# Third attention stage of an eight-stage transformer kernel: the causal mask as two constant rows in the stacked operands and four 64x64 triangle products, in place of one 128-row mask product

## The chip, the cores and the metric

One core of one Trainium2 chip runs the whole program. The metric is the device time of one execution in microseconds (us). Engines are named as the profile names them: PE is the matrix engine (TensorE), PEld its weight loads, DVE the vector engine, ACT the scalar engine, POOL GpSimd, SP the engine that issues the DMAs.

## The reference, cut to what matters

The reference is four layers, each an attention and a feed-forward part with modulated layer norms, over 16 batches of 256 tokens with 256 features. The change touches the attention of the second layer (`L1_attn`, the third of eight stages), a differential attention with 32 score heads of 8 features:

```python
q = (x @ Wq).reshape(b, t, 2 * H, HD).transpose(0, 2, 1, 3) * scaling
k = (x @ Wk).reshape(b, t, 2 * H, HD).transpose(0, 2, 1, 3)
scores = jnp.einsum('bhqd,bhkd->bhqk', q, k)
causal = jnp.triu(jnp.full((t, t), -jnp.inf, dtype=jnp.float32), 1)
aw = jax.nn.softmax((scores + causal).astype(jnp.float32), axis=-1)
lam = jnp.exp(jnp.sum(lq1 * lk1)) - jnp.exp(jnp.sum(lq2 * lk2)) + LAMBDA_INIT
aw = aw.reshape(b, H, 2, t, t)
aw = aw[:, :, 0] - lam * aw[:, :, 1]
attn = jnp.einsum('bhqk,bhkd->bhqd', aw, v)
```

## The kernel before, in words

The eight stages run one after another, each over the 16 batches, in software-pipelined slots (`slots`). Each engine has its own program, and semaphores order them. A slot i of this stage holds on PE the maxima of batch i, most of the exponentials' scores of batch i - 1, and projections, transposes and the output product of neighbouring batches.

**Stacks.** q and k are split into three bf16 parts. `l1a_sync` writes the parts to DRAM, `l1a_stack_sync` reads them back into `QS` and `KS` (per parity of the batch) as 48 rows for one half of the heads, on partitions 0 to 47, and 48 for the other half, on partitions 64 to 111. One bf16 product over 48 rows gives an f32-like score. Three more rows of `QS` take the row maxima (negated, in three bf16 parts), against ones in `KS`; `l1a_max_sync` sends them there from `maxT`, in two halves of a batch. The other rows are zero in `QS`.

**Pairs.** Scores are worked on in pairs of PSUM banks of 512 columns: bank `pr` = 0 takes its operands from partitions 0 to 63, bank 1 from 64 to 127. Each batch has 12 maxima pairs (`max_pair(b, o, n)`, o = 0 to 3, n = 0 to 2, written Mon here, as M00 or M32) and 12 exponential pairs (`exp_pair`, Eon). A pair is either four blocks of 128 columns a bank (M with n = 0, E with n = 2: "wide mask", since a mask of 512 columns goes over the bank) or two blocks of 256 columns a bank (all the others: "narrow mask", 256 columns). The mask is a product of the identity (`ident_b`, 128x128) with `later4` or `earlier4` (a 128x128 triangle of -1e30, repeated), added to the bank in PSUM. In a wide pair it comes ahead of the scores, in a narrow one behind them. So a narrow pair has on PE 4 score matmuls and 2 mask matmuls, a wide pair 2 mask matmuls and 8 score matmuls.

**Who frees whom.** The three banks 1 to 3 serve M pairs, 4 to 6 E pairs. DVE reduces each M bank to maxima (`maxima`, L2185); ACT takes the exponential of each E bank (`exps`, L2104). An M pair waits on PE until DVE has done the first bank of the M pair before it; an E pair waits until ACT has done the first bank of the E pair before it. E00 and E20 wait for the maxima's rows (`max_ready`), M00 for the stacks (`stack_ready`).

**PE's order in a slot** is written by hand in `slot` of `l1a_tensor`. V is `values` (products on column strips of 32), P a projection, bt a transpose by token, nT and MT other transposes:

M00, E12, P(k), E20, M01, V1, E21, M02, E22, P(q), E30, M10, V2, E31, M11, E32, M12, nT, M20, V3, MT first, M21, M22, P(v), bt 0 to 2, M30, bt 3, out, E00, M31, E01, M32, E02, next tokens' transposes, E10, V0, MT second, E11, and the next slot.

**Other orders.** ACT: between E12 and E20 it evicts k (L2118, L2119), between E20 and E21 it copies V1's result (`l_oT`, L2110), and so on; between E02 and E10 it writes the next `hT` (L517); ahead of E11 it copies V0's result and `maxT` (L2093). DVE: behind M22 comes `by_token` (L2193, L2195) and `subtract`, then M30, the gated output (L533), M31, M32. POOL makes the parts of q, k and of the maxima. SP's slot order is `l1a_sync(i + 1)`, maxima's first half of i, stacks of i + 1, maxima's second half of i. `l1a_pads`, which POOL runs in the second stage's first four slots, sets the constant rows by memset and counts `a_zero` to 4.

Of the kernel before, what the change touches and what calls it, by code (L numbers as in the profile page):

```python
# [16 lines left out]
P = 128  # L17
B = 16
T = 256
# [119 lines left out]
def layout(**inputs):  # L139

    a = {k: np.asarray(v) for k, v in inputs.items()}
    f = np.float32
    k = np.arange(P)
    two = lambda w: np.ascontiguousarray(w.reshape(KH, P, -1).transpose(1, 0, 2))
    out = {"x": a["L0_attn_x"].reshape(B, TT, P, D)}
    out["c"] = np.ascontiguousarray(np.stack([two(a[f"L{i}_c"].T) for i in range(LAYERS)], 1))
    out["wmod"] = np.stack([a[f"L{i}_wmod"] for i in range(LAYERS)])
    ident = np.eye(P, dtype=f)
    out["ident"] = ident

    for n in "qkvo":
        out[f"l0_w{n}"] = two(a[f"L0_attn_W{n}"])
    out["l0_wg1"], out["l0_wg2"] = two(a["L0_attn_Wg1"]), a["L0_attn_Wg2"]
    ld = a["L0_attn_log_decay"]
    out["l0_ld"] = ld
    out["l0_nw"] = np.ascontiguousarray(a["L0_attn_norm_w"].reshape(KH, P).T)
    age = np.arange(T)[None, :] - k[:, None]
    out["l0_age"] = np.maximum(age, 0).astype(f)
    out["causal"] = (age >= 0).astype(f)
    out["l0_side"] = (k[:, None] // HD % 2 == np.arange(2)[None, :]).astype(f)  # L160
    age = age[:, 0:P]

    pad = np.zeros((FT * P - INTER, D), np.int32)
    down = np.concatenate([a["L0_ffn_down_idx"].T, pad]).reshape(FT, P, D).transpose(1, 0, 2)
    out["l0_idx"] = np.concatenate([two(a["L0_ffn_gate_idx"].T).reshape(P, -1), two(a["L0_ffn_up_idx"].T).reshape(P, -1),
                                    down.reshape(P, -1)], 1)
    out["l0_lut"] = a["L0_ffn_lut"]

    out["l2_b"] = two(a["L2_attn_B"].T)
    out["l2_c"] = np.ascontiguousarray(a["L2_attn_C"].T)  # L170
    out["l2_d"] = np.ascontiguousarray(a["L2_attn_D"].reshape(KH, P).T)

    out["l3_wqkv"], out["l3_wo"] = two(a["L3_attn_w_qkv"]), two(a["L3_attn_w_out"])
    out["l3_dec"] = np.ascontiguousarray(np.repeat(a["L3_attn_decay_param"], HD).reshape(KH, P).T)
    out["l3_head"] = (k[:, None] // HD == np.arange(P // HD)[None, :]).astype(f)

    for n in "qkvo":
        w = a[f"L1_attn_W{n}"]
        if n in "qk":
            w = w.reshape(D, 8, KH, 2, 8).transpose(0, 2, 3, 4, 1).reshape(D, D)  # L180
        out[f"l1_w{n}"] = two(w)
    out["lam_v"] = np.stack([np.stack([a[f"L1_attn_lq{i}"], a[f"L1_attn_lk{i}"]]) for i in (1, 2)])
    bf = mybir.dt.np(BF16)
    low = np.where(age < 0, np.float32(LOW), np.float32(0))
    out["ident_b"] = ident.astype(bf)
    out["later4"] = np.ascontiguousarray(np.broadcast_to(low.T[:, None], (P, 4, P))).astype(bf)
    out["earlier4"] = np.ascontiguousarray(np.broadcast_to(low[:, None], (P, 4, P))).astype(bf)

    out["l1_we"] = np.ascontiguousarray(a["L1_ffn_expert_w"].reshape(E, KH, P, D).transpose(2, 1, 0, 3))
    out["l1_gw"], out["l1_eb"] = two(a["L1_ffn_gate_w"].T), a["L1_ffn_expert_b"]  # L190

    out["l2_la"], out["l2_w"] = two(a["L2_ffn_lora_A"].reshape(P, D).T), two(a["L2_ffn_weight"].T)
    out["l2_rw"] = two(a["L2_ffn_router_w"].T)
    out["l2_lb"] = np.ascontiguousarray(a["L2_ffn_lora_B"].transpose(0, 2, 1)).reshape(P, D)
    out["l2_sel"] = (np.arange(E)[:, None] == k[None, :] // (P // E)).astype(f)

    rows = lambda w: w.transpose(1, 0, 2).reshape(D, NS)
    out["l3_sw"] = two(rows(a["L3_ffn_select_weight"]))
    out["l3_up"] = two(np.concatenate([rows(a["L3_ffn_lora_update"]), np.zeros((D, E), f)], 1))
    out["l3_md"], out["l3_db"], out["l3_mdr"] = two(a["L3_ffn_select_mean_diff"].T), two(a["L3_ffn_debias_w"].T), a["L3_ffn_select_mean_diff"]  # L200
    out["l3_cs"] = np.stack([a["L3_ffn_imp_center"], a["L3_ffn_imp_slope"]], 1)
    out["l3_dg"] = np.concatenate([a["L3_ffn_lora_degen"].transpose(0, 2, 1).reshape(NS, D), a["L3_ffn_bias_w"]])
    blk = (np.arange(NS)[:, None] // (NS // E) == np.arange(E)[None, :]).astype(f)
    out["l3_blk"] = np.concatenate([blk, np.zeros((P - NS, E), f)])
    out["l3_own"] = np.concatenate([blk, np.zeros((E, E), f)])
    out["l3_e72"] = np.ascontiguousarray(np.concatenate([blk, np.eye(E, dtype=f)]).T)
    out["l3_tail"] = (np.arange(NS + E) >= NS).astype(f)[:, None]
    out["l3_one"] = np.ones((P, E), f)
    out["rank"] = np.broadcast_to(np.arange(E, 0, -1).astype(f), (P, TT, E)).copy()
    return {"in_" + k: v for k, v in out.items()}  # L210


def build(nc, ins, y_out, first=0, last=8):
    ctx = ExitStack()
    with ctx:
# [1614 lines left out]
        def l1a_tensor(pe, pl, s):  # L1830
            psum_free(pe, pl)
            pe.wait_ge(w_in[2], 16 * len(weights[2]))
            pe.wait_ge(setup["a_wo"], 1)
            pe.wait_ge(setup["a_zero"], 4)

# [29 lines left out]
            def half_rows(x, pr, g, a, b_, rows):  # L1867
                return x[64 * pr:64 * pr + rows, g, a:b_]

            def max_pair(b, o, n):  # L1870
                u = 6 * o + 2 * n
                q, k = QS[b.par], KS[b.par]
# [5 lines left out]
                    pe.wait_ge(*s.max(b - 1, 23))  # L1878
                banks = [bank(1 + (u + pr) % 3) for pr in range(2)]
                if n == 0:  # L1880
                    for pr in range(2):
                        pe.matmul(banks[pr], ident_b[:, :], later4[:, :, :], start=True, stop=False)
                    for j in range(4):
                        for pr in range(2):
                            last_ = pe.matmul(banks[pr][:, j * P:(j + 1) * P], half_rows(q, pr, 4 * o + j, 0, P, M_ROW),  # L1885
                                              half_rows(k, pr, 4 * o + j, 0, P, M_ROW), start=False, stop=j == 3)
                            if j == 3:
                                last_.then_inc(s.max_ps.sem, 1)
                else:
                    for j in range(2):  # L1890
                        for pr in range(2):
                            g = 4 * o + 2 * (n - 1) + j
                            pe.matmul(banks[pr][:, j * T:(j + 1) * T], half_rows(q, pr, g, P, T, M_ROW),  # L1893
                                      half_rows(k, pr, g, 0, T, M_ROW), start=j == 0, stop=False)
                    for pr in range(2):
                        pe.matmul(banks[pr].rearrange("p (j k) -> p j k", j=2)[:, :, P:T], ident_b[:, :], later4[:, 0:2, :],  # L1896
                                  start=False, stop=True).then_inc(s.max_ps.sem, 1)

            def max_T(b, half_):
                pe.wait_ge(*s.mparts(b, half_ + 1))  # L1900
# [21 lines left out]
            def exp_pair(b, o, n):  # L1922
# [11 lines left out]
                if n < 2:  # L1934
                    for j in range(2):
                        for pr in range(2):
                            g = 4 * o + 2 * n + j
                            pe.matmul(banks[pr][:, j * T:(j + 1) * T], half_rows(k, pr, g, 0, P, 64),  # L1938
                                      half_rows(q, pr, g, 0, T, 64), start=j == 0, stop=False)
                    for pr in range(2):  # L1940
                        pe.matmul(banks[pr].rearrange("p (j q) -> p j q", j=2)[:, :, 0:P], ident_b[:, :], earlier4[:, 0:2, :],  # L1941
                                  start=False, stop=True).then_inc(s.score.sem, 1)
                else:
                    for pr in range(2):
                        pe.matmul(banks[pr], ident_b[:, :], earlier4[:, :, :], start=True, stop=False)  # L1945
                    for j in range(4):
                        for pr in range(2):
                            last_ = pe.matmul(banks[pr][:, j * P:(j + 1) * P], half_rows(k, pr, 4 * o + j, P, T, 64),
                                              half_rows(q, pr, 4 * o + j, P, T, 64), start=False, stop=j == 3)
                            if j == 3:  # L1950
                                last_.then_inc(s.score.sem, 1)

            def values(b, o):
                pe.wait_ge(*s.prob(b, 6 * o + 6))
# [371 lines left out]
            slots(pool, slot, -3, LOOP2, B + 1)  # L2326

        N_STACK = 4
        M_ROW = 8 * N_TERMS

        def l1a_sync(sp, pl, s, b):

# [9 lines left out]
        def l1a_stack_sync(sp, pl, s, i):  # L2342
# [5 lines left out]
            for c in (1, 0):  # L2348
                if not c or not (i - 1).ok:
                    sp.wait_ge(*scratch_ready(i, c))  # L2350
                for r in range(2):
                    to = (QS, KS)[c][i.par][64 * r:64 * r + M_ROW, :, :].rearrange("p g t -> p (g t)")
                    sp.dma_start(to, qk_dram[i.par, c, r].rearrange("n (d g) x -> (n d) (g x)", d=8)).then_inc(stack_in[i.par], 16)

        def l1a_max_sync(sp, pl, s, b, half_):
# [109 lines left out]
        def _(sp):  # L2465
# [20 lines left out]
            for p in range(first, last):  # L2486
                pl = p - first
                def slot(i):
                    if i.ok and p != 2:
                        gate_load(sp, pl, sigs[pl], i)  # L2490
                    if i.reg is None and i.off == 1 and pl + 1 < len(sigs):
                        if pl:
                            sp.wait_ge(*sigs[pl - 1].x(Idx(None, B - 1)))
# [70 lines left out]
```

## Time and profile before

| | |
|---|---|
| median of 3 runs | 2099.39 us (2097.16 to 2099.85) |
| profiled execution | 2101.8 us, its span in the trace 2100.0 us |
| mean granted PE clock | 0.936 of full speed |
| busy: PE, DVE, ACT, POOL | 1850.9, 1373.0, 741.1, 895.8 us |
| the third stage | score products from 670 to 1235 us of the span |

The profile is one execution. A busy time is a sum over the span; PE's is modelled, since matmuls are pipelined and a single one takes longer than its share of a stream, so what a group of matmuls costs is read from the start of one group to the start of the next. The timeline merges neighbouring instructions of one kind on one row, with their count.

### The profile page before, as it was taken

What the parts mean: (1) busy time and instruction counts of PE and PEld (TensorE: products, weight loads), DVE (VectorE), ACT (ScalarE), POOL (GpSimd) and SP (SyncE); (2) the same over time, 40 slices, a digit from 0 to 9 for tenths busy, and PEclk for the clock granted to TensorE, in tenths of its full rate; (3) what the DMA queues carried; (4) which work ended last, traced back from release to release, by engine and by line L of the source; (5) the groups of instructions that cost most, each with busy time, mean ns of one, the idle gap of its engine ahead of it and who ended that gap; (6) DMA issues with size and microseconds to landing.
All of it is one profiled execution on the core that took longest, in us unless ns stands there. A gap on an engine that the chain in (4) does not pass through costs nothing.

```text
span 2100.0 us, 40010 instructions
## 1 busy us (share of the span) xinstructions
PE 1850.9 (88%) x13400; PEld 1270.9 (61%) x13400; DVE 1373.0 (65%) x3587; ACT 741.1 (35%) x1511; POOL 895.8 (43%) x965
## 2 busy tenths in 40 slices
PE   8999999689995999999999968998967888998887
PEld 5555555489993455555555436676756666885443
DVE  4767677465552556565656537888845776886775
ACT  2544444112221465555555531111122223443332
POOL 0345454565653254545454332233333223663233
PEclk7999999799998999999999988999999888999887
DMA  6100000100003745454545300000011000000111
GB/s 230 52 9 5 7 5 9 31 9 8 10 10 68 158 87 106 89 103 90 100 89 103 68 11 9 9 7 7 10 33 43 15 13 17 14 16 13 35 37 40
DMA packets 68177, 93.34 MB, mean 44 GB/s; under 512 B 9852, under 2 KB 62316, under 8 KB 64748
## 3 DMA queue, kind: packets, MB, share of 16 engines
q1 hardware_dynamic: 68076, 92.01, 19.3%
q8 instruction: 61, 1.00, 0.2%
q14 instruction: 40, 0.33, 0.1%
HBM read 61.70 MB, written 29.49 MB: 43 GB/s over the span
## 4 chain that ended last, share of the span: by engine, by line
PE 68%; DVE 19%; issue 6%; POOL 2%; ACT 2%; DMA 2%; SPq 1%; DVEq 1%; POOLq 0%; ACTq 0%
PE PS L1020 16%; PE PS L1965 3%; PE PS L668 3%; PE PS L1841 3%; PE PS L725 3%; PE PS L1175 3%; DVE negmax L2185 2%; PE PS L741 2%; PE PS L507 2%; DVE xn L497 2%; PE PS L722 2%; PE PS L1893 2%; PE PS L1896 2%; PE PS L1945 1%; PE PS L1938 1%
## 5 line engine op out<-in xcount | busy, mean ns | idle before, releaser
L2185 DVE TENSOR_REDUCE negmax<-PS 128x2 f32<-128x512 f32 (+1 forms) x384 | 246.9, 684 | 211.2 <-PE PS L1885 106.0
L538 POOL TENSOR_TENSOR X<-X,y_sb 128x512 f32 (+1 forms) x128 | 165.2, 1291 | 150.1 <-DVE y_sb L533 145.1
L533 DVE TENSOR_TENSOR y_sb<-PS,ga_sb 128x512 f32<-128x512 f32 x96 | 66.2, 690 | 179.0 <-PE PS L769 50.1
L1020 PE MATMUL PS<-we_hi,h_parts 128*128 128x512 f32 x512 | 179.7, 412 | 0.0
L497 DVE TENSOR_SCALAR xn<-X,mv,rs 128x256 f32 (+1 forms) x256 | 155.3, 648 | 22.4 <-POOL rs L490 21.2
L517 ACT ACTIVATE hT<-PS,modT 128x256 f32<-128x256 f32 x256 | 130.0, 559 | 105.6 <-PE PS L507 104.6
L2104 ACT ACTIVATE pw<-PS 128x512 f32<-128x512 f32 x256 | 139.0, 600 | 75.2 <-PE PS L1941 75.2
L488 POOL TENSOR_TENSOR rs<-mv,eps 128x2 f32<-128x2 f32 x128 | 26.6, 208 | 296.3 <-DVE mv L481 296.1
L1020 PE MATMUL PS<-l_h_parts,lut_hi 128*128 128x256 f32 (+1 forms) x768 | 145.5, 291 | 6.7 <-POOL l_h_parts L1143 6.7
L1509 DVE SCALAR_TENSOR_TENSOR l_acc<-PS,rt_g,l_acc 128x256 f32<-128x256 f32 x256 | 106.1, 475 | 30.6 <-PE PS L1020 25.5
L1020 PEld LDWEIGHTS PS<-l_h_parts,lut_hi 128*128 128x128 f32 (+1 forms) x768 | 117.8, 184 | 9.6 <-issue 5.4
L1020 PEld LDWEIGHTS PS<-we_hi,h_parts 128*128 128x128 f32 x512 | 99.1, 194 | 26.5 <-issue 5.9
L1020 PE MATMUL PS<-l_h_parts,lut_lo 128*128 128x256 f32 (+1 forms) x384 | 110.3, 287 | 0.0
L507 PE MATMUL PS<-ident,xn 128*128 128x128 f32 x512 | 82.1, 284 | 31.6 <-DVE xn L497 30.8
L1020 PE MATMUL PS<-we_lo,h_parts 128*128 128x512 f32 x256 | 102.9, 402 | 0.0
L1175 PE MATMUL PS<-hT,l_wqkv 128*128 128x256 f32 x384 | 94.3, 397 | 4.9 <-ACT hT L517 4.0
L1089 ACT ACTIVATE l0f_act<-PS 128x256 f32<-128x256 f32 x96 | 36.8, 383 | 175.1 <-PE PS L1020 175.1
L490 POOL TENSOR_TENSOR rs<-rs,half 128x2 f32<-128x2 f32 x128 | 94.0, 734 | 10.0
L476 DVE BATCH_NORM_STATS2 st<-X 128x6 f32 (+1 forms) x256 | 95.1, 413 | 1.1 <-DMA X<-in_x 0.9
L1152 POOL TENSOR_TENSOR l0f_hid_parts<-l0f_hid,l0f_hid_parts 128x256 fp32r<-128x256 f32 x96 | 72.2, 753 | 50.5 <-DVE l0f_hid_parts L1014 50.0
L507 PEld LDWEIGHTS PS<-ident,xn 128*128 128x128 f32 x512 | 58.4, 143 | 57.0 <-DVE xn L497 38.5
L988 POOL TENSOR_TENSOR l_ms<-l_ms,half 128x32 f32<-128x32 f32 x16 | 87.1, 5442 | 1.3
(270 smaller groups left out, 4383.2 us busy)
## 6 DMA issues: line engine op xcount, KB each, us to landing
ga_sb<-ga_dram SPq DMA_DIRECT2D x128, 128.0 KB, 2.9
qk_dram<-qk_parts SPq DMA_DIRECT2D x64, 192.0 KB, 2.8
KS<-qk_dram SPq DMA_DIRECT2D x32, 384.0 KB, 5.7
QS<-qk_dram SPq DMA_DIRECT2D x32, 384.0 KB, 9.5
qk_dram<-qk_parts SPq DMA_DIRECT2D x64, 128.0 KB, 2.8
wmod<-in_wmod SPq DMA_DIRECT2D x4, 1536.0 KB, 14.0
qk_dram<-qk_parts SPq DMA_DIRECT2D x64, 64.0 KB, 2.5
y_out<-X SPq DMA_DIRECT2D x16, 256.0 KB, 2.2
```

Of the source, the lines that this page charges most:

```text
L476: last_ = dve.bn_stats(st6[b.par][:, t, :], xb(b)[:, t, :])
L490: pool.tensor_tensor(rs[b.par][:, :], rs[b.par][:, :], half[:, 0:TT], ALU.pow).then_inc(s.rstd.sem, 1)
L497: last_ = dve.tensor_scalar(xn[b.par][:, t, :], xb(b)[:, t, :], mv[b.par][:, t, 0:1], rs[b.par][:, t:t + 1], ALU.subtract, ALU.mult)
L507: last_ = pe.transpose(PS[:, 0, kh * T + t * P:kh * T + (t + 1) * P], xn[b.par][:, t, kh * P:(kh + 1) * P], ident[:, :])
L517: last_ = act.activation(hT[b.par][:, kh, :], PS[:, 0, kh * T:(kh + 1) * T], ACT.Identity, bias=modT[:, sub, 0, kh, bass.ds(b.n, 1)], scal ...
L538: pool.tensor_tensor(xb(b), xb(b), y_sb[b.par][:, :, :], ALU.add).then_inc(s.x.sem, 1)
L988: pool.tensor_tensor(ms_sb[:, :], ms_sb[:, :], half[:, 0:TT * HEADS], ALU.pow).then_inc(s.rn.sem, 1)
L1020: last_ = pe.matmul(out, x.bitcast(F32R), y.bitcast(F32R), start=start and n == 0, stop=stop and n == 2)
L1175: last_ = pe.matmul(bank(1 + n)[:, m * T:(m + 1) * T], l3_wqkv[:, kh, n * D + m * P:n * D + (m + 1) * P], hT[b.par][:, kh, :], start=kh == ...
L1509: dve.scalar_tensor_tensor(l1_acc[b.par][:, t, :], bank(1 + (2 * q + t) % 4)[:, e * D:(e + 1) * D], rt_g[b.par][:, t, x_:x_ + 1], l1_acc[b ...
L2104: act.activation(to.rearrange("p a n -> p (a n)"), bank(4 + (2 * n + pr) % 3), ACT.Exp).then_inc(s.prob.sem, 1)
L2185: dve.tensor_reduce(to, src, AX.X, ALU.max, negate=True).then_inc(s.max.sem, 1)
```

## The change

The stacks get two constant rows below the 48 (rows 48 and 49 of each half). Row t of `QS` is 1 in the first 64 tokens of token tile t, row t of `KS` is -1e30 in the last 64 tokens of it. So the score product itself masks the upper right 64x64 block of each 128x128 diagonal block. `M_ROW` grows from 48 to 50, and the maxima's three rows move down by two. What is left to mask are the two 64x64 triangles on the diagonal. `triangles` adds them with four matmuls a pair, each of 64 rows by 64 columns of the array, with the identity's diagonal quarter as weights: quarter 0 for bank 0 and quarter 1 for bank 1, then quarter 1 for bank 0 and quarter 0 for bank 1. They come behind the scores in every pair. The rows are sent by eight DMAs (`l1a_cut_sync`) from SP's queue in the second stage, at the slot of batch 14, into both parities; PE waits for them (`a_pad`) at the head of the third stage.

```diff
+    cut_q, cut_k = np.zeros((2, HEADS, T), f), np.zeros((2, HEADS, T), f)
+    for t in range(TT):
+        cut_q[t, :, t * P:t * P + P // 2] = 1
+        cut_k[t, :, t * P + P // 2:(t + 1) * P] = LOW
+    out["cut"] = np.stack([cut_q, cut_k]).astype(bf)
...
             pe.wait_ge(setup["a_zero"], 4)
+            pe.wait_ge(setup["a_pad"], 16 * 8)
...
+            def triangles(banks, tri, n, done):
+                for half_ in range(2):
+                    for pr in range(2):
+                        h = pr ^ half_
+                        r0, r1 = 64 * h, 64 * h + 64
+                        last_ = pe.matmul(banks[pr][r0:r1, :, r0:r1], ident_b[r0:r1, r0:r1], tri[r0:r1, 0:n, r0:r1],
+                                          start=False, stop=True)
+                        if half_ == 1:
+                            last_.then_inc(done.sem, 1)
...
                 if n == 0:
-                    for pr in range(2):
-                        pe.matmul(banks[pr], ident_b[:, :], later4[:, :, :], start=True, stop=False)
                     for j in range(4):
                         for pr in range(2):
-                            last_ = pe.matmul(banks[pr][:, j * P:(j + 1) * P], half_rows(q, pr, 4 * o + j, 0, P, M_ROW),
-                                              half_rows(k, pr, 4 * o + j, 0, P, M_ROW), start=False, stop=j == 3)
-                            if j == 3:
-                                last_.then_inc(s.max_ps.sem, 1)
+                            pe.matmul(banks[pr][:, j * P:(j + 1) * P], half_rows(q, pr, 4 * o + j, 0, P, M_ROW),
+                                      half_rows(k, pr, 4 * o + j, 0, P, M_ROW), start=j == 0, stop=False)
+                    triangles([x.rearrange("p (j k) -> p j k", j=4) for x in banks], later4, 4, s.max_ps)
...
-                    for pr in range(2):
-                        pe.matmul(banks[pr].rearrange("p (j k) -> p j k", j=2)[:, :, P:T], ident_b[:, :], later4[:, 0:2, :],
-                                  start=False, stop=True).then_inc(s.max_ps.sem, 1)
+                    triangles([x.rearrange("p (j k) -> p j k", j=2)[:, :, P:T] for x in banks], later4, 2, s.max_ps)
...
-        M_ROW = 8 * N_TERMS
+        S_ROW = 8 * N_TERMS
+        M_ROW = S_ROW + TT
+        def l1a_cut_sync(sp):
+            sp.wait_ge(setup["a_zero"], 4)
+            for i in range(2):
+                for c, to in enumerate((QS, KS)):
+                    for r in range(2):
+                        sp.dma_start(to[i][64 * r + S_ROW:64 * r + M_ROW, :, :], ins["cut"][c]).then_inc(setup["a_pad"], 16)
...
+                    if i.reg is None and i.off == B - 2 and p == 1:
+                        l1a_cut_sync(sp)
```

`exp_pair` is changed in the same way, with `earlier4` and the first 128 of each 256 columns.

## Rows read from the trace of the kernel before

**Rows 1.** Busy time in a stretch of 40 us: start:end, length, each engine's, clock, DMA

```profile
1000.00:1040.00 40.00, 38.67 (x403) 23.18 (x402) 25.61 (x54) 20.06 (x39) 17.49 (x20) 1.00 0.54 103
```

**Rows 2.** Waits of PE, 700 to 1200 us: total us, times, longest

```profile
PE PS L1893 <- DVE negmax L2185: 14.2, 28, 0.7
PE PS L1882 <- DVE negmax L2185: 3.8, 14, 0.7
```

**Rows 3.** Timeline of the eviction of q and k, two slots apart

```profile
843.22 0.60 ACT L2118 ACTIVATE qk<-PS 128x512 f32<-128x512 f32 x1 [0.99 <-PE PS L1841]
...
912.84 0.60 ACT L2118 ACTIVATE qk<-PS 128x512 f32<-128x512 f32 x1 [0.99 <-PE PS L1841]
```

**Rows 4.** PE's groups by shape, whole span: count, busy us, mean ns, idle before

```profile
L1896 PE MATMUL PS<-later,ident_b 128*128 128x256 bf16 x256 | 51.0, 282 | 0.0
...
L1882 PE MATMUL PS<-later,ident_b 128*128 128x512 bf16 x128 | 39.6, 392 | 22.0 <-DMA QS<-qk_dram 17.3 <-DVE negmax L2185 4.7
```

**Rows 5.** Timeline of PE, one slot: start us, length us, instructions

```profile
1008.87 0.59 PE L1945 MATMUL PS<-earlier,ident_b 128*128 128x512 bf16 x2
...
1013.11 0.39 PE L1941 MATMUL PS<-earlier,ident_b 128*128 128x256 bf16 x2
1013.34 0.59 PE L1882 MATMUL PS<-later,ident_b 128*128 128x512 bf16 x2
1013.87 0.40 PE L1885 MATMUL PS<-KS,QS 48*128 48x128 bf16 x8
1014.20 0.61 PE L1945 MATMUL PS<-earlier,ident_b 128*128 128x512 bf16 x2
...
1018.96 0.61 PE L1965 MATMUL PS<-pw,l_vpad 128*32 128x256 f32 x8
1019.39 0.40 PE L1967 MATMUL PS<-pz,l_vpad 128*32 128x128 f32 x8
1019.73 0.39 PE L1938 MATMUL PS<-QS,KS 64*128 64x256 bf16 x4
1020.05 0.39 PE L1941 MATMUL PS<-earlier,ident_b 128*128 128x256 bf16 x2
...
1021.02 0.61 PE L1945 MATMUL PS<-earlier,ident_b 128*128 128x512 bf16 x2
...
1032.63 0.39 PE L1893 MATMUL PS<-KS,QS 48*128 48x256 bf16 x4
...
1034.03 0.39 PE L1893 MATMUL PS<-KS,QS 48*128 48x256 bf16 x4 [0.68 <-DVE negmax L2185]
```

**Rows 6.** Weight loads by shape, whole span, columns as before

```profile
L1643 PEld LDWEIGHTS PS<-hT,l_sw 128*64 128x64 f32 x64 | 7.9, 144 | 12.9 <-issue 8.1 <-DVE l_c L1739 2.0 <-ACT hT L517 0.4
...
L1896 PEld LDWEIGHTS PS<-later,ident_b 128*128 128x128 bf16 x256 | 14.6, 97 | 27.8 <-issue 27.8
...
L1685 PEld LDWEIGHTS PS<-l_sq,l_blk 128*8 128x8 f32 x32 | 1.6, 90 | 7.5 <-issue 7.4
```

**Rows 7.** Timeline, the first weight loads of V1

```profile
1018.28 0.16 PEld L1965 LDWEIGHTS PS<-pw,l_vpad 128*32 128x32 f32 x8 [0.21 <-issue]
```

**Rows 8.** The chain that ended last, in order of time: start us, us

```profile
1004.37 0.27 DVE l_rl L2193
...
1007.58 0.69 DVE negmax L2185
1008.32 0.39 PE PS L1893 x4
...
1009.84 0.59 ACT pz L2104
1010.48 0.39 PE PS L1938 x4
```

**Rows 9.** Timeline of ACT in the same slot

```profile
1020.37 1.08 ACT L2104 ACTIVATE pw<-PS 128x512 f32<-128x512 f32 x2
```

**Rows 10.** Timeline of PE where the stage runs out

```profile
1224.20 0.39 PE L1938 MATMUL PS<-QS,KS 64*128 64x256 bf16 x4 [1.66 <-DMA QS<-maxT]
```

More of the change, by code:

```diff
@@ L1939, in exp_pair @@
                                       half_rows(q, pr, g, 0, T, 64), start=j == 0, stop=False)
-                    for pr in range(2):
-                        pe.matmul(banks[pr].rearrange("p (j q) -> p j q", j=2)[:, :, 0:P], ident_b[:, :], earlier4[:, 0:2, :],
-                                  start=False, stop=True).then_inc(s.score.sem, 1)
-                else:
-                    for pr in range(2):
-                        pe.matmul(banks[pr], ident_b[:, :], earlier4[:, :, :], start=True, stop=False)
+                    triangles([x.rearrange("p (j q) -> p j q", j=2)[:, :, 0:P] for x in banks], earlier4, 2, s.score)
+                else:
                     for j in range(4):
                         for pr in range(2):
[L1948 to L1951, printed above, removed]
+                            pe.matmul(banks[pr][:, j * P:(j + 1) * P], half_rows(k, pr, 4 * o + j, P, T, 64),
+                                      half_rows(q, pr, 4 * o + j, P, T, 64), start=j == 0, stop=False)
+                    triangles([x.rearrange("p (j q) -> p j q", j=4) for x in banks], earlier4, 4, s.score)
             def values(b, o):
@@ L2351, in l1a_stack_sync @@
                 for r in range(2):
-                    to = (QS, KS)[c][i.par][64 * r:64 * r + M_ROW, :, :].rearrange("p g t -> p (g t)")
+                    to = (QS, KS)[c][i.par][64 * r:64 * r + S_ROW, :, :].rearrange("p g t -> p (g t)")
                     sp.dma_start(to, qk_dram[i.par, c, r].rearrange("n (d g) x -> (n d) (g x)", d=8)).then_inc(stack_in[i.par], 16)
```

## The prediction

> **What bounds the kernel now.** I read first the table of stages over time. In a stretch of the third stage PE is busy 38.67 of 40 us, at full granted clock, DVE 25.6, ACT 20.1, POOL 17.5 [rows 1]. So this stage runs at PE's pace, unlike what an average over eight stages would tell, and work taken off PE can be worth time. Next the list of waits: between 700 and 1200 us the maxima's pairs wait for DVE 14.2 + 3.8 = 18.0 us in 42 places [rows 2], 1.3 us for each of some 14 batches. These waits are where a faster PE will lose part of its gain. Then the distance of one instruction over two slots: 912.84 - 843.22 = 69.62, so a batch takes 34.81 us [rows 3]. There are 16 batches, and 15 slots (1 to 15) hold both a full set of M pairs and a full set of E pairs.
>
> **What one pair costs on PE.** The mean of a mask product (282 and 392 ns, [rows 4]; as many again stand for `earlier4`) holds the array's latency. What it costs in a stream is the distance of starts [rows 5]. Narrow mask, then wide mask, both on the full array: 13.34 - 13.11 = 0.23 us, which I take as 0.22. Wide mask, then scores: 13.87 - 13.34 = 0.53. Eight 128-column scores, then a mask: 14.20 - 13.87 = 0.33. Four 256-column scores, then a mask: 20.05 - 19.73 = 0.32. Now 0.22 us for 2 x 256 columns is 2.4 GHz, so 2 x 512 columns are 0.43 and the 0.53 holds 0.10 to 0.11 more; the scores' 0.33 is 0.22 (half their columns, since the two 64-row halves run at once) and again 0.11. In the values' products, which use four strips of 32 columns, a second group starts after 0.43 (19.39 - 18.96, same shape), and scores behind them after 0.34, 0.12 more than their own 0.22. So each change of the array's split costs 0.11 us, and staying in one costs nothing. This is the term that speaks against the change.
>
> Before: a narrow pair is 0.22 + 0.11 + 0.22 = 0.55, and 0.11 more if the next group does not use the full array. A wide pair is 0.43 + 0.11 + 0.22 = 0.76, and 0.11 more if the next is not a score group.
>
> After: the scores are unchanged (50 rows of weights instead of 48 change no column). The triangles are four matmuls of 128 (narrow) or 256 columns (wide). If the two on different quarters run at once, each pair takes two steps: 0.11 or 0.22 us. No row shows a split in both directions; rows show it by rows (scores) and by columns (values: four strips, [rows 5]), so I take it. Their weights have 64 columns in bf16, for which there is no row either. Bounds: a bf16 load of 128 columns has 97 ns, an f32 load of 64 columns 144 [rows 6]. So the first, which nothing hides, costs 0 to 0.05 more; later ones run beside matmuls. I take 0.02, nearer the bf16 row. A narrow pair then is 0.22 + 0.11 + 0.11 + 0.02 + 0.11 = 0.57, say 0.56, a wide one 0.67, always with the change at its end, because triangles are followed by something else everywhere.
>
> So on PE a narrow pair gains 0.09, but loses 0.01 where the mask ran on into a full-array group (E11, M02, E30, M11, M12, M22, M32: seven of sixteen). A wide one gains 0.19 (eight a batch; E32, ahead of M12, 0.08). M20 and M30 also get 0.11 of a new change in front, behind nT and bt. PE's work falls by 9 x 0.09 - 7 x 0.01 + 7 x 0.19 + 0.08 - 0.22 = 1.93 us a batch. By plain columns it would have been 16 x 0.11 + 8 x 0.21 = 3.4.
>
> **What of it reaches the end.** I go through PE's order and ask at each pair which wait ends last.
> - bt 3 to M32: a chain on DVE. The last token transposes are read at 1004.37; by_token, subtract, two M30 maxima, the gated output and the first of M31 follow back to back, until 1007.58 + 0.69, and M32 starts at 1008.32 [rows 8]. PE only has out and three pairs in these 3.95 us. E00, M31, E01: nothing gained.
> - M32: -0.01. E02 to E10: bank 0's exponential starts 0.97 behind E02 (1009.84 - 1008.87, [rows 8, 5]) and E10 0.64 later. With triangles bank 0 is ready after 0.22 + 0.11 + 0.02 + 0.11 (its second triangle's start) + 0.33 for latency and hand-over (before, its last score started at 0.43 + 0.11 + 0.16 = 0.70 and 0.27 followed; a product twice as long adds 0.05), 0.79. Gain 0.18.
> - E10, E11, M00: from E02's exponentials ACT runs without a gap (two of E02, `hT`, two of E10, V0's copy, `maxT`) up to E11's, and E12 waits for the first of these. Nothing.
> - E12: 0.19. E20 and M01: 0.09 each.
> - E21, M02: V1's copy holds up E21's exponential till 1020.37, 0.64 behind E21 [rows 9, 5]; 0.60 later the wide E22 may start, and did, at 1021.02. Nothing.
> - E22: 0.19. E30: -0.01. M10: 0.19.
> - E31, M11, E32: the same copy, nothing; then E32's 0.08 to 0.11, I take 0.11 with M11's earlier start for M12.
> - M12, nT to M20: M20 waits for M12's first reduction as M22 does for M21's below; nothing. M20: 0.19.
> - M21 to M22: 34.03 - 32.63 = 1.40 [rows 5]: bank 0 ready (0.65), one reduction (0.69), hand-over. Bank 0 is as late as before, since its second triangle is third in order (0.22 + 0.11 + 0.02 + 0.05 and latency, before 0.22 + 0.11 + 0.11). Nothing.
> - M22: -0.01. M30: 0.19 - 0.11 = 0.08.
>
> Sum: -0.01 + 0.18 + 0.19 + 0.18 + 0.19 - 0.01 + 0.19 + 0.11 + 0.19 - 0.01 + 0.08 = 1.28 us a batch, two thirds of PE's 1.93. Times 15 slots: 19.2. Slots 0 and 16 hold only M or only E pairs and wait for DVE and ACT; a few wide pairs there lead such a chain, 0.2 each and 0.4 where the clock is half: 1.3 us. Together 20.5 us.
>
> **What is added elsewhere.** Eight DMA issues of 16 KB on SP at the second stage's batch 14. Even at 1 us each they hold SP for 8 us; behind them stands only the gate load of batch 15, which has to wait for DVE's output of an earlier batch anyway, and then SP has nothing to issue until the first q and k parts. `a_zero` was counted up in slots 0 to 3 of that stage. Lower bound 0, upper bound 1 us if batch 15's gate came late; I take 0. PE's wait on `a_pad` is met tens of us before. 48 more matmuls and 48 more loads a batch: eight loads and eight matmuls already pass in 0.22 us [rows 5], so issue does not bind. E20 waits for `maxT`'s rows by DMA: where the stage runs out it stood 1.66 us for them [rows 10], in steady slots not. E12's gain brings E20 nearer to them; if it is lost there, 0.19 x 15 = 3 us. The bound for the forecast's range.
>
> Against the profiled execution: 2101.8 - 20.5 = 2081.3. Its time is 2.4 above the median of the runs, so the forecast is 2099.4 - 20.5 = 2079. Own range: no cost of the first load gives 0.02 x 17 places more, -26, 2074; its upper bound takes 0.03 x 17 = 0.5 a batch away, -12, and E20's 3 us more, 2090.
>
> **The rivals.**
> (a) Loads set the pace of a quarter. A 64-column f32 load takes 144 - 90 = 54 ns longer than one of 8 columns [rows 6]. If bf16 loads on quarters cost as much and run one behind another, each group of triangles takes 4 x 0.054 = 0.22 us or more: narrow pairs lose 0.02 (or 0.12), wide ones gain 0.15, and bank 0 is ready 0.1 us later in the six chains that wait for it. Summed over the same places this is -0.07 us a batch: 2100, no change. For it: nothing shows a bf16 load on part of the columns. Against it: V1's first eight loads, on four strips, span 0.16 us together [rows 7] where one alone takes 90 ns or more [rows 6], so the other seven start within 0.07 us and loads on different strips overlap. The Trainium skill, page TensorEngine Tiling (Array Packing), section Restrictions, says that column tiling turns off fast weight load, and its page TensorE: Matmul & The Clock Gate, section LDWEIGHTS, gives a load as columns / 1.2 GHz, by which four loads in a row are an estimated 213 ns. By that rule without overlap the sum would be that of this rival; if the loads overlap, that of the forecast. No row here shows bf16 loads of this shape.
> (b) Slower: the four triangles don't run at once. Then they take 0.22 and 0.43 us, what the full masks took, and nothing pays for the ten more changes of split a batch (60 for 50). A narrow pair is 0.66, a wide one 0.87 to 0.89. Gains turn to losses of 0.02 to 0.14 at the places above (0.11 where the mask ran on, and 0.11 each in front of M20 and M30 where these don't wait), and bank 0 is ready 0.07 later: 1.1 us a batch, 16 us, 2116. It decides for slower as soon as the second and third triangle's overlap is less than about half of the columns. For it: quarter 1 is used twice in a row, quarter 0 only at the ends, and bank 0 gets its second triangle while its first may still be draining. The Trainium skill, the same tiling page, section Restrictions and Gotchas, says that different row tiles must not use one PSUM bank at a time; the order here is meant for that, and no row shows the case.
> (c) The change from scores to triangles is free, as both keep 64-row halves. Then each pair drops another 0.11, and 0.11 at each of 14 places where scores follow triangles. On the path: 1.9 us a batch more, 3.1 in all, 2051. For it only that no row shows such a change; all that rows show cost 0.11.
>
> **Chances.** Forecast 0.70 (with E20's DMA and dearer first loads in it), (a) 0.10, (b) 0.12, (c) 0.08. The range leaves out (b) and (c), 0.20, and takes in (a): 2062 to 2101. The lower end lies below the forecast's own 2074, for a case between it and (c). A measurement of this kernel tells about 0.2%, 4 us, from no change. Faster: 0.70 + 0.08 = 0.78; the same 0.10; slower 0.12.
>
> **What would show it.** Triangles in the timeline: x4 with the next group 0.22 to 0.25 us (narrow) or 0.33 to 0.36 (wide) behind them is the forecast; 0.33 and 0.53 is (b); 0.33 to 0.37 for both is (a); scores to triangles in 0.22 is (c). The eviction of q and k repeats after 67.1 us for two slots instead of 69.6. PE's waits for DVE between 700 and 1200 us grow from 18 to some 23, and waits for ACT ahead of E12, E22 and E32 appear. PE's busy share falls. M21 to M22 stays 1.40, bt 3 to M32 3.95. The forecast goes wrong if triangles are serial, if waits for DMA at E20 or M00 grow past 1 us, or if the thinner work lets the granted clock fall below 1.00 between 720 and 1200 us.

## The result, and the profile after

The changed kernel takes 2105.99 us (median of 12 runs, 2101.78 to 2112.04) against 2098.07 us for the kernel before in the same session (12 runs). The ratio is 1.0041, 95% interval 1.0028 to 1.0054: slower by 0.4%, where 1.0% faster was forecast. The profiled execution has a span of 2110.1 us.

PE's timeline of a slot of the changed kernel comes first (start, length, instructions); it answers to [rows 5].

```profile
1000.64 0.41 PE L1883 MATMUL PS<-later,ident_b 64*64 64x256 bf16 x4
1000.98 0.64 PE L1973 MATMUL PS<-pw,l_vpad 128*32 128x256 f32 x8
...
1002.42 0.39 PE L1951 MATMUL PS<-QS,KS 64*128 64x256 bf16 x4
1002.74 0.30 PE L1883 MATMUL PS<-earlier,ident_b 64*64 64x128 bf16 x4
1002.97 0.39 PE L1908 MATMUL PS<-KS,QS 50*128 50x256 bf16 x4
1003.29 0.30 PE L1883 MATMUL PS<-later,ident_b 64*64 64x128 bf16 x4
1003.73 0.40 PE L1957 MATMUL PS<-QS,KS 64*128 64x128 bf16 x8
...
1008.12 0.39 PE L1908 MATMUL PS<-KS,QS 50*128 50x256 bf16 x4
...
1009.53 0.39 PE L1908 MATMUL PS<-KS,QS 50*128 50x256 bf16 x4 [0.79 <-DVE negmax L2193]
...
1013.98 0.66 PE L1986 MATMUL PS<-ident,l_oT 128*128 128x128 f32 x4
...
1018.63 0.39 PE L1908 MATMUL PS<-KS,QS 50*128 50x256 bf16 x4 [0.40 <-DVE negmax L2193]
...
1019.19 0.40 PE L1957 MATMUL PS<-QS,KS 64*128 64x128 bf16 x8
...
1020.61 0.39 PE L1951 MATMUL PS<-QS,KS 64*128 64x256 bf16 x4
```

Four wide triangles with the change of split behind them take 0.34 us (1000.98 - 1000.64), four narrow ones 0.23 (1002.97 - 1002.74), scores before triangles 0.32 (1002.74 - 1002.42). So the quarters do run at once, as the forecast had it. E21 to E22 is 1.31 (1003.73 - 1002.42), M21 to M22 1.41 (1009.53 - 1008.12), E02 to E10 1.42 (1020.61 - 1019.19): also as forecast. From bt 3 to M32 PE takes 4.65 us (1018.63 - 1013.98). The kernel before has these two rows, which give 4.64:

```profile
1003.68 0.65 PE L1978 MATMUL PS<-ident,l_oT 128*128 128x128 f32 x4
...
1008.32 0.39 PE L1893 MATMUL PS<-KS,QS 48*128 48x256 bf16 x4 [0.31 <-DVE negmax L2185]
```

The loads of the triangles, from the table of groups by shape, answer to [rows 6]; the second row shows the four loads of one group in the timeline:

```profile
L1883 PEld LDWEIGHTS PS<-later,ident_b 64*64 64x64 bf16 x768 | 26.9, 106 | 35.6 <-issue 29.2
...
1002.74 0.14 PEld L1883 LDWEIGHTS PS<-earlier,ident_b 64*64 64x64 bf16 x4 [0.21 <-issue]
```

A 64-column bf16 load has 106 ns, 9 more than a full one (in a stretch at full clock, 780 to 870 us, 104 against 97). Now the same timeline 20 us further on, at the jump from the second slot of PE's loop back to the first (M00 is the first pair of the loop body), and the table of stretches for the slots before and across such a jump, whose last columns are clock, DMA share and GB/s:

```profile
1023.14 0.30 PE L1883 MATMUL PS<-earlier,ident_b 64*64 64x128 bf16 x4
1026.24 0.40 PE L1901 MATMUL PS<-KS,QS 50*128 50x128 bf16 x8 [2.80 <-issue]
1026.57 0.41 PE L1883 MATMUL PS<-later,ident_b 64*64 64x256 bf16 x3
1030.31 0.37 PE L1883 MATMUL PS<-later,ident_b 64*64 64x256 bf16 x1 [3.33 <-issue]
1030.61 0.61 PE L1957 MATMUL PS<-QS,KS 64*128 64x128 bf16 x8
1031.14 0.64 PE L1883 MATMUL PS<-earlier,ident_b 64*64 64x256 bf16 x4
1031.71 3.29 PE L1847 MATMUL PS<-hT,l_wk 128*128 128x256 f32 x8
```

```profile
809.65:843.11 33.46, 31.46 (x416) 19.09 (x412) 21.97 (x43) 19.50 (x38) 17.47 (x21) 1.00 0.52 101
843.11:884.91 41.80, 33.71 (x416) 20.27 (x412) 22.04 (x43) 19.51 (x39) 18.86 (x23) 0.92 0.43 84
```

Both stretches run from one eviction of k to the next. A slot without a jump takes 33.46 us, against 34.81 before [rows 3] and 33.53 forecast. A slot behind a jump takes 41.80, 8.34 more. Of this, 2.80 + 3.33 = 6.13 us are two pauses of PE which wait for nothing that the profile shows ("issue"): one at the jump's target, the other in the middle of a group of four triangles, ahead of its last one. Of the other 2.2 us, 1.3 are seen in the projection of k, which takes 3.29 us where without a jump it takes 1.99: the granted clock behind the pauses is lower (0.92 over the slot). The list of PE's waits, 700 to 1200 us, answers to [rows 2]:

```profile
PE PS L1908 <- DVE negmax L2193: 16.9, 28, 0.8
PE PS L1883 <- issue: 9.7, 3, 3.3
PE PS L1901 <- issue: 8.8, 3, 3.2
PE PS L1901 <- DVE negmax L2193: 3.4, 14, 0.8
PE PS L1901 <- DMA QS<-qk_dram: 1.4, 1, 1.4
```

Three times two pauses, and PE's loop over slots 4 to 11 in two-slot bodies jumps back three times. Three jumps cost about 3 x 8.34 = 25 us (the three slots take 41.80, 41.74 and 41.62). None of the waits of the kernel before was of this kind and length. What PE waits for is seen in the table of DMA queues. From 885 to 1095 us it has this row for the kernel before:

```profile
q8 instruction: 1, 0.02, 0.0%
```

and this one for the changed kernel:

```profile
q8 instruction: 24, 0.39, 0.8%
```

The queue that brings instructions (packets, MB, share) moved one packet of 16 KB in this stretch for the kernel before, and even that one starts at 1087.5 us, behind the loop's last pass, which ends at 1082.9. In the changed kernel it moved 24, nine of them in the round from 947 to 1023 us. In 14 us around the pauses above, 1020 to 1034 us, it is three:

```profile
q8 instruction: 3, 0.05, 1.6%
```

Two of the three lie in the pauses. They start at 1023.6 and 1028.0 us and take 1.0 us each, and PE goes on 1.7 and 1.3 us behind their ends, at 1026.24 and 1030.31.

So in the kernel before PE held its loop body of two slots and did not fetch it again. The change adds 2 matmuls and 2 loads to each of the 24 pairs of a slot, 192 instructions to the body of two slots. From then on PE fetches its body in every round, and stands still at the jump until the first pieces are there. The Trainium skill, page Runtime: NRT & Kernel Launch, section Instruction fetch mechanics, says that PE's instruction memory holds 2048 instructions, is refilled in blocks of 16 KiB or 256 instructions, and that a taken branch to a target outside the current window of two such pages forces a fetch before execution can go on. The packets of 16 KB and the pauses at the jump agree with it. The two pages do not: the kernel before jumps back over some 1560 instructions, and no packet moves. Nor is a body of 1757 held, although it is shorter than 2048; the experiments below narrow the limit down.

### The profile page after: what moved, and what is told of

It is laid out like the page before. It is cut to its first block, busy times and chain, and to the rows that moved or that the text cites. A ratio compares the mean times of both kernels' runs of the same rounds, so it can differ in the third digit from the quotient of the medians.

```text
span 2110.1 us, 41555 instructions
## 1 busy us (share of the span) xinstructions
PE 1829.3 (87%) x14168; PEld 1278.6 (61%) x14168; DVE 1375.5 (65%) x3587; ACT 741.9 (35%) x1511; POOL 895.3 (42%) x965
## 4 chain that ended last, share of the span: by engine, by line
PE 64%; DVE 19%; issue 7%; ACT 4%; POOL 2%; DMA 2%; SPq 1%; DVEq 1%; ACTq 0%; POOLq 0%
PE PS L1025 16%; PE PS L1883 4%; PE PS L1847 3%; PE PS L673 3%; PE PS L1973 3%; PE PS L1180 3%; PE PS L730 3%; DVE negmax L2193 2%; PE PS L746 2%; PE PS L512 2%; PE PS L727 2%; DVE xn L502 2%; PE PS L697 1%; ACT pw L2112 1%; PE PS L774 1%
```

## The experiments

Throughout, "body" is PE's loop body of two slots. By the built program it has 1565 PE instructions before and 1757 after the change, if a bf16 product or a transpose counts as a load and a matmul, any other f32 product as two of each, and every register or semaphore instruction as one. Three fused register instructions are counted together with their 8 parts; counted once each, they make it 1557 and 1749. This count serves for differences; it need not be what the memory holds to the instruction.

**PE's loop written out (u_after, u_before).** The same edit on the changed kernel and on the kernel before:

```diff
-            slots(pe, slot, -2, LOOP2, B + 1)
+            for i in range(-2, B + 2):
+                slot(Idx(None, i))
```

> The changed kernel, with PE's loop over the slots 4 to 11 of the third stage written out (20 slots in a row, no jump; the other engines keep their loops). Theory (code): PE's loop body of two slots has grown by 192 instructions, is no longer held, and is fetched again at each of three jumps back, about 8.3 us each (41.8 against 33.5 us from one eviction of k to the next). Then the pauses of 2.8 and 3.3 us go away everywhere, no slot takes longer than 33.6 us, and the time falls by some 25 us against the changed kernel: 2080 us, 0.991 of the kernel before. Rival (split): the pauses come from the 64x64 split or the order of the triangles; they stay wherever they were, since the instructions and their order are the same: 2106. Rival (clock): the clock falls by itself now and then under thinner work: time stays above 2095.

> The kernel before, with PE's loop of the third stage written out in the same way. Theory (code): its body was held and the jump back showed no pause, so nothing is gained: 2098 us, within 0.2% of the kernel before; 34.8 us a slot. Rival: the loop itself (register arithmetic for the waits, the jump) already cost something, then this is faster by what it cost, and the part of it in the other run's gain is not the larger body's.

Measured: the changed kernel without PE's loop 2084.68 us, ratio to the kernel before 0.9927 (0.9900 to 0.9954), 21 us below the changed kernel (24.4 between the stages of the two profiles, where 25 were expected). The kernel before without PE's loop 2097.70 us, ratio 0.9997 (0.9983 to 1.0011). In u_after's waits between 640 and 1260 us the long pauses are gone; the one "issue" entry that is left stood in the kernel before too:

```profile
PE PS L1908 <- DVE negmax L2194: 22.5, 38, 0.8
PE PS L1901 <- DMA QS<-qk_dram: 18.6, 3, 16.7
...
PE PS L1951 <- issue: 0.9, 1, 0.9
```

The same triangles in the same order make no pause when there is no jump, so neither the split nor the clock by itself is the cause. In the kernel before, the loop as such cost nothing that can be measured.

**The instructions without the triangles (cut_before).** The kernel before, each mask product in two halves, in both kinds of pair and for maxima and exponentials; here for the wide maxima pairs:

```diff
-                    for pr in range(2):
-                        pe.matmul(banks[pr], ident_b[:, :], later4[:, :, :], start=True, stop=False)
+                    for h in range(2):
+                        for pr in range(2):
+                            pe.matmul(banks[pr][:, h * T:(h + 1) * T], ident_b[:, :], later4[:, 2 * h:2 * h + 2, :],
+                                      start=h == 0, stop=False)
```

> The kernel before, with each mask product cut in two of half the columns: the same columns on the full array, no triangles, no constant rows, but four mask products a pair and so the same number of PE instructions in the loop body as in the changed kernel. Theory (code): three jumps back with two pauses of about 3 us each and some half clock behind them, 20 to 25 us slower than the kernel before: 2118 to 2123 us. Rival (split): without a 64x64 split there is no pause and the time stays at 2098 to 2100.

Measured: 2123.24 us, ratio 1.0113 (1.0088 to 1.0137), 25 us slower than before. PE's timeline at one of its jumps:

```profile
955.03 0.40 PE L1946 MATMUL PS<-earlier,ident_b 128*128 128x128 bf16 x4
958.16 1.03 PE L1883 MATMUL PS<-later,ident_b 128*128 128x256 bf16 x4 [2.74 <-issue]
959.13 0.61 PE L1887 MATMUL PS<-KS,QS 48*128 48x128 bf16 x8
962.29 1.03 PE L1952 MATMUL PS<-earlier,ident_b 128*128 128x256 bf16 x4 [2.55 <-issue]
```

Full-array products, no constant rows, no new DMA: the same two pauses, at the jump's target and twelve products behind it (eleven in the changed kernel), in a body that is as long. This run decides for the code.

**How long the body may be (wide_only, cut_few).** In wide_only, the changed kernel's narrow pairs get the full mask back (cut to `max_pair`; the same in `exp_pair`):

```diff
-                    triangles([x.rearrange("p (j k) -> p j k", j=2)[:, :, P:T] for x in banks], later4, 2, s.max_ps)
+                    for pr in range(2):
+                        pe.matmul(banks[pr].rearrange("p (j k) -> p j k", j=2)[:, :, P:T], ident_b[:, :], later4[:, 0:2, :],
+                                  start=False, stop=True).then_inc(s.max_ps.sem, 1)
```

> The changed kernel with triangles in the wide pairs only (8 a batch); the narrow pairs add the full 256-column mask product as before (the constant rows mask their block a second time). The loop body has 64 instructions more than before instead of 192. Theory (code): if the limit lies above that, there is no pause, and the wide pairs bring their 1.0 us a batch, 15 us in all: 2083 us. If the limit lies below, the same three pauses: 2108. Rival (split): pauses appear with the wide triangles too (in the changed kernel the second pause stood ahead of the last triangle of a wide pair): 2108.

cut_few is cut_before with the cut in the wide maxima pairs alone (the diff above and nothing else).

> The kernel before, with only the masks of the four wide maxima pairs a batch cut in two: 32 instructions more in the loop body than before, where 64 more (wide triangles only) gave the full pauses. Theory (code) with a limit at the body's size: either no pause, 2098 us, and the limit lies between 32 and 64 more, or the full three, 2122, and it lies within 32 of the kernel before. A gradual price would show as something between, 2102 to 2108.

Measured: wide_only 2109.75 us, ratio 1.0052 (1.0035 to 1.0069), with six pauses:

```profile
PE PS L1901 <- issue: 18.3, 6, 3.5
```

cut_few 2099.88 us, ratio 1.0002 (0.9986 to 1.0019), with one instruction packet between 885 and 1095 us. So 32 instructions more are free and 64 more cost all three jumps: it is a step, between 1597 and 1629 in the count above, and no gradual price. The kernel before lay 2 to 4% below it. In wide_only a slot without a jump takes 33.86 us: the wide triangles bring 0.95 us a batch, the narrow ones 0.40.

Length is not all in which these bodies differ, and the second pause shows it. In the changed kernel it stands behind the eleventh product of M00, in wide_only behind the third:

```profile
949.44 0.28 PE L1901 MATMUL PS<-KS,QS 50*128 50x128 bf16 x3 [2.87 <-issue]
953.23 0.48 PE L1901 MATMUL PS<-KS,QS 50*128 50x128 bf16 x5 [3.51 <-issue]
```

That is 8 products or 16 instructions earlier. By the built programs wide_only's body begins 240 instructions earlier too, because the slots ahead of the loop carry the same edit. 240 + 16 = 256, so the second pause fits a border between pieces of 256 instructions, one packet each. From this border each body's place can be worked out (an estimate; with the fused instructions counted once). The bodies of before, cut_few and cut_outside (below) touch seven pieces, the latter two with room for 9 and 5 instructions more; those of wide_only, cut_before and the changed kernel touch eight. So the limit may be one of length, or one of seven pieces, in which the place where the body begins counts as well. No run separates the two.

**Where the body lies (cut_outside).** As cut_before, but the masks are cut only in the slots that are written out (one line of the edit; it sets in how many parts a mask is added):

```diff
+        CUT = CUT_E = lambda b: 2 if b.reg is None else 1
```

> The kernel before, with all masks cut in two as in the run that had the pauses, but only in the slots outside the loop; the loop body is as long as before and lies elsewhere in the program. Theory (the size of the body decides): no pause at the jumps, 2098 to 2100 us. Rival (where the body lies, or the length of the whole program): pauses at the jumps, above 2110 us.

Measured: 2099.88 us, ratio 1.0008 (0.9989 to 1.0026), 2 instruction packets in the stretch where cut_before has 24. So the program's length does not decide, nor does this shift of the body's place, by some 100 instructions within its pieces. It still leaves the body in seven of them.

**One jump (one_jump).** The changed kernel with

```diff
-            slots(pe, slot, -2, LOOP2, B + 1)
+            slots(pe, slot, -2, (4, 8), B + 1)
```

> The changed kernel with PE's loop over the slots 4 to 7 only and the other slots written out: the same large body, one jump back instead of three. Theory (code): each jump back costs 8.3 us, so this stands one jump above the kernel without a loop (2084.7) and two below the changed kernel (2106): 2089 to 2093 us, pauses at one place only, at about 870 us of the span. Rival (something else that the long loop brings, such as DMA traffic over the stage): not in steps of one jump; several pauses or none.

Measured: 2090.80 us, ratio 0.9959 (0.9941 to 0.9976), and one set of pauses in PE's timeline:

```profile
874.58 0.40 PE L1901 MATMUL PS<-KS,QS 50*128 50x128 bf16 x8 [3.23 <-issue]
...
878.10 0.37 PE L1883 MATMUL PS<-later,ident_b 64*64 64x256 bf16 x1 [2.79 <-issue]
```

Without a jump 2084.7, with one 2090.8, with three 2106.0: 6 to 8 us each. The slot with the jump takes 42.02 us, 8.6 more than the one before it.

**Which triangles are worth it (u_wide, u_mix).** u_after gained 14 to 15 us where 20.5 were forecast. From the first eviction of k to that of batch 3 it takes 96.92 us, the kernel before 94.27. wide_only took only 92.29. So two more kernels, both with PE's loop written out: u_wide has wide triangles only, u_mix narrow ones too, but not in the first three batches (cut to `max_pair`; the same in `exp_pair`):

```diff
+                    if b.off < 3:
+                        for pr in range(2):
+                            pe.matmul(banks[pr].rearrange("p (j k) -> p j k", j=2)[:, :, P:T], ident_b[:, :], later4[:, 0:2, :],
+                                      start=False, stop=True).then_inc(s.max_ps.sem, 1)
+                        return
```

> The changed kernel with triangles in the wide pairs only and PE's loop written out. With the loop this kernel showed 33.86 us a slot (all triangles: 33.46), and reached batch 3 some 4.6 us earlier than the kernels with all triangles did, where the first slots ran partly at half clock. If both stay: no pauses, 0.40 x 12 slots dearer and 4.6 cheaper than all triangles without a loop, so about the same, 2084 us. If the narrow triangles are worth what PE saved on them by columns alone, it stands 10 us or more above, 2095.

> As the run before, but with narrow triangles too from batch 3 on; batches 0 to 2 have the full narrow masks. Theory (the first slots' loss comes from the narrow triangles there: PE catches up with the DMA of the stacks and with DVE, waits, and its clock falls): it keeps the 4.6 us at the start and the 33.46 us a slot: about 2080 us, 4 us below all triangles without a loop. Rival (the loss at the start is chance of the clock): the same as all triangles, 2084.

Measured: u_wide 2079.74 us, ratio 0.9911 (0.9893 to 0.9929); u_mix 2082.38 us, ratio 0.9913 (0.9891 to 0.9936). Both beat the kernel before by 0.9% and the changed kernel by more; between them and u_after the intervals don't decide. From the first eviction of k to the last transposes by token the profiles take 593.8 us before, 603.6 in the changed kernel, 579.2 in u_after, 577.8 in u_wide, 576.1 in u_mix. Each is one execution, so the order of the last three is not shown. Up to batch 3 u_mix needs 92.6 us, as forecast, and its slots take 33.45. Over all profiles this start takes 96.9 to 97.3 us in the three kernels with narrow triangles in it (the changed kernel, one_jump, u_after), 92.3 to 93.1 in the three with wide ones alone there, and 93.6 to 95.4 in the five without triangles. The 4 us are thus the narrow triangles of the first batches. The rows bear on how they come about, but do not settle it: in the first slots PE waits for the stacks' DMA and for DVE anyway, and the granted clock falls to 0.68 of full speed in u_after and one_jump (the level of 1.2 GHz for part of the stretch), and to 0.73 in the changed kernel, where u_mix and u_wide stay at 1.00. It was 1.00 in the kernel before, but 0.83 in u_before and cut_few, which have no triangles either. The table of stretches, for u_after:

```profile
726.00:736.00 10.00, 8.19 (x89) 4.04 (x88) 6.71 (x15) 5.21 (x10) 4.74 (x7) 0.68 0.55 95
```

and for the kernel before:

```profile
726.00:736.00 10.00, 8.39 (x99) 3.74 (x97) 6.90 (x17) 6.78 (x14) 4.84 (x7) 1.00 0.64 103
```

and for u_mix:

```profile
726.00:736.00 10.00, 9.01 (x113) 4.53 (x114) 7.39 (x16) 7.43 (x16) 5.75 (x7) 1.00 0.52 86
```

## Why the prediction was wrong

- **The step that failed** is "48 more matmuls and 48 more loads a batch: eight loads and eight matmuls already pass in 0.22 us [rows 5], so issue does not bind." The rate was right: no group of triangles is held up within a slot. But the instructions were costed only by their rate, at nothing, and they also have a length. The loop body grew past what PE holds, and three jumps cost 25 us (41.80 - 33.46 each). With this term the forecast of -20.5 us becomes +4.5; measured are +8 by the medians and +9.8 between the stages of the two profiles, and the rest is what the start and the end of the stage did not bring (below). The clue stood in the trace of before: one instruction packet in 210 us, against one every 8 to 18 us in the slots written out. A loop that is not fetched again is a resource, and nobody asked how full it was.
- **Quarters at once, change of split at 0.11 us: right.** 0.23 and 0.34 us for triangles with the change behind them, 0.32 for scores. Rivals (a), (b) and (c) are all refuted by these rows: (b) needed 0.33 and 0.53, (a) 0.33 and more for both, (c) scores at 0.22. For (a) the bf16 load of 64 columns was the open price: 106 ns, and four loads of a group span 0.14 us, so they overlap. The Trainium skill, page TensorEngine Tiling (Array Packing), section Restrictions, says that column tiling turns off fast weight load. The 9 ns more may come from that, which no run here shows; the rival that was built on it needed loads one behind another, and the 0.14 us refute it.
- **What of a steady slot's gain reaches the end: right within 0.1 us.** A slot was to fall from 34.81 to 33.53; it falls to 33.46 (33.48 as the mean of 12 slots in u_after). The places that DVE and ACT were to hold are held: M21 to M22 1.41, E21 to E22 1.31, bt 3 to M32 unchanged. From M02's triangles to E22 it is 0.44 us (1003.73 - 1003.29), of which the triangles need 0.23: the wait for ACT that was forecast there, too short for the list of waits. PE's wait for DVE grew from 18.0 to 20.3 us, where some 23 were forecast; in u_after, where no pause stands in its place, it is 22.4.
- **The start and the end of the stage: wrong.** Of the 20.5 us, 15.4 belong to the twelve slots from batch 3's eviction of k to batch 15's; in u_after these gained 15.9. The other 5.1 were to come ahead of them and behind them; there 2.65 were lost (94.27 against 96.92 us) and 1.3 gained. The sum took the steady slot for slot 1 and the last two, where other waits end last and, at the start, the clock is not full. This is a term that was mis-sized; it would not have turned the sign.
- **DMAs, SP, `a_pad`: right.** Nothing waits for the new ones, and in the steady slots E20's DMA did not take E12's gain. The stacks' DMA does hold up M00 of batch 1, for 1.4 us in the changed kernel and 0.15 before; u_before, without any triangle, has 1.2 there.
- **The range** (2062 to 2101) missed the result by 5 us. The side on which it failed had a chance, 0.12, but by another mechanism: it was one to do with the array, and the loss came from fetching the instructions.

## What to carry to other kernels

Count the instructions of a loop body on each engine as one counts bytes of a buffer, and read the instruction queue in the profile before adding any: if it is silent during the loop, the body is held, and an edit that adds instructions may end that with one step. If it must grow, write the loop out on that one engine. To buy only the part of the edit that pays (here wide pairs: 70% of a slot's gain for a third of the instructions) helps only if the rest stays under the step: wide_only, with 64 instructions more, paid for all three jumps. A gain worked out for the steady slot does not hold for the first ones, where other waits end last.

## What the runs showed of the hardware

- What PE holds of a loop has a step: with 1597 instructions (by the count above) in the body no packet is fetched in the loop, with 1629 each round fetches some nine packets of 16 KB. Whether the place of the body plays a part is open. Each jump back then costs two pauses of 2.4 to 3.5 us, each ending 1.3 to 1.8 us behind a packet, and makes its slot 6.6 to 9.2 us longer, with the lower clock behind them.
- Code that runs straight on is fetched without a pause that shows: 21 packets between 885 and 1095 us in u_after, and no wait of PE on "issue" in which the kernel before had none.
- The array runs two 64x64 products on diagonal quarters at once: four matmuls of 256 columns in 0.34 us with the change of split included. A change of split costs about 0.11 us wherever the rows show one between 128x128, 64x128, 64x64 and 128x32 (an estimate: the time from one group's start to the next, such as 0.23 or 0.34 us for narrow or wide triangles, less the 0.11 or 0.21 that their columns take at 2.4 GHz).
